# A retention block between two MoE layers: the second MoE's front moves into the last retention tiles

## The reference

```
x = x + 0.5 * moe(layernorm(x))                # MoE "a"
x = x + attn(layernorm(x))                     # retention, two layers
x = x + 0.5 * moe(layernorm(x))                # MoE "b", the same weights as "a"

moe(h): probs = softmax(h @ router_w + bias); top 2 of 16, weights normalised to sum 1
        15 experts: silu(h @ gate_w[e]) * (h @ up_w[e]) @ down_w[e]; the 16th gives h itself
        shared = silu(conv3(h)) * (h @ shared_up) @ shared_down    # causal, 3 taps
        returns shared + routed
attn(x): twice: x += retention(layernorm(x)) gated by silu, projected out
                x += gelu(layernorm(x) @ ffn1 + b1) @ ffn2 + b2
         then a final layernorm with gain and bias
```

## Time and profile before

| | |
|---|---|
| median of 3 runs | 1481.09 us (1480.42 to 1487.93) |
| profiled execution | 1481.23 us, of which span 1479.1 us |
| busy in the span | PE 1323.7 us (89%), DVE 1018.2 (69%), POOL 636.3 (43%), ACT 597.0 (40%) |
| mean granted clock of TensorE | 0.96 |

### The profile page before, as it was taken

How to read it: one execution, slowest core, us unless ns; L and a number is a source line. 1 busy time by engine, 2 the same in 40 slices (tenths; PEclk the granted TensorE clock), 3 DMA queues, 4 the chain that set the end, 5 groups by cost and what they waited for, 6 DMA issues and landing times. The chain is left out here.

```text
span 1479.1 us, 30591 instructions
## 1 busy us (share of the span) xinstructions
PE 1323.7 (89%) x11824; PEld 1086.4 (73%) x11824; DVE 1018.2 (69%) x2373; ACT 597.0 (40%) x1009; POOL 636.3 (43%) x509
## 2 busy tenths in 40 slices
PE   3899999658999999999998999999999849899994
PEld 2468996346878878888887887887887724799952
DVE  5854564768778778778768778778867667546634
ACT  6325665211443343443442433334334462356620
POOL 4766413722333134224334334633643466746045
PEclk9899999768999999999999999999999969999997
DMA  9987765710000000001010000000000051668544
GB/s 333 362 280 247 235 206 187 231 37 1 2 1 2 1 2 1 2 2 33 8 37 28 1 2 16 16 1 16 16 15 2 29 186 68 221 232 249 166 154 138
DMA packets 109323, 139.18 MB, mean 94 GB/s; under 512 B 11776, under 2 KB 95616, under 8 KB 109184
## 3 DMA queue, kind: packets, MB, share of 16 engines
q1 hardware_dynamic: 94784, 101.56, 21.1%
q0 software_dynamic: 12288, 33.57, 6.8%
q10 hardware_dynamic: 2112, 2.10, 0.4%
HBM read 71.66 MB, written 65.54 MB: 93 GB/s over the span
## 5 line engine op out<-in xcount | busy, mean ns | idle before, releaser
L1624 DVE TENSOR_TENSOR l_probs<-l_banks,l_past 128x512 f32<-128x512 f32 x256 | 159.9, 681 | 34.3 <-PE l_banks L1850 34.2
L1478 POOL TENSOR_TENSOR l_g_lo<-l_q,l_g_hi 128x1024 fp32r<-128x1024 f32 x16 | 38.4, 2398 | 285.1 <-ACT l_g_hi L1390 285.1
L1399 ACT ACTIVATE l_act_f<-l_w_ps,l_ffn_b 128x512 f32<-128x512 f32 x120 | 82.7, 689 | 176.2 <-PE l_w_ps L81 170.5
L79 PE MATMUL l_w_ps<-l_w_hi,l_f_hi 128*128 128x256 f32 x496 | 142.9, 288 | 3.6 <-DVE l_f_lo L1655 2.2
L80 PE MATMUL l_w_ps<-l_w_lo,l_f_hi 128*128 128x256 f32 x496 | 138.5, 279 | 0.0
L81 PE MATMUL l_w_ps<-l_w_hi,l_f_lo 128*128 128x256 f32 x496 | 138.4, 279 | 0.0
L597 POOL DMA_INDIRECT a_picked<-rows,a_pos_i x64 | 65.4, 1022 | 90.9 <-issue 68.4
L1465 POOL TENSOR_TENSOR l_q_wide<-l_q,l_pair_mask 128x1024 f32<-128x1024 f32 x32 | 60.1, 1898 | 100.5 <-DVE l_q L1602 100.5
L1655 DVE TENSOR_TENSOR l_f_lo<-l_act_f,l_f_hi 128x512 fp32r<-128x512 f32 x128 | 86.3, 703 | 24.1 <-ACT l_f_hi L1400 24.1
L79 PE MATMUL l_w_ps<-l_b_hi,l_w_hi 128*128 128x512 f32 x240 | 102.7, 428 | 0.0
L597 POOL DMA_INDIRECT b_picked<-rows,b_pos_i x64 | 61.5, 961 | 93.8 <-issue 68.5
(11 more groups left out here) (400 smaller groups left out, 4057.5 us busy)
## 6 DMA issues: line engine op xcount, KB each, us to landing
rows<-a_zeros SPq DMA_DIRECT2D x15, 1024.0 KB, 13.6
a_xb<-rows SPq DMA_DIRECT2D x46, 256.0 KB, 3.1
rows<-a_yb SPq DMA_DIRECT2D x46, 256.0 KB, 3.1
b_xb<-rows SPq DMA_DIRECT2D x46, 256.0 KB, 3.4
rows<-b_yb SPq DMA_DIRECT2D x46, 256.0 KB
a_w_in<-in_moe_w SPq DMA_DIRECT2D x15, 384.0 KB, 12.8
b_w_in<-in_moe_w SPq DMA_DIRECT2D x15, 384.0 KB, 9.5
l_w<-in_ffn_w SPq DMA_DIRECT2D x8, 512.0 KB, 6.4
```

The lines of the kernel that those rows point to most:

```text
L79: tensor.matmul(out, w_hi, x_hi, start=start, stop=False)
L1399: nc.scalar.activation(act_f[:, f, :], hidden_ps(b, f), ACT.Gelu, bias=ffn1_b[:, b.layer, f:f + 1]).then_inc(act_done, 1)
L1624: dve.tensor_tensor(probs[c % 2][:, r * w:(r + 1) * w].rearrange("p (h n) -> p h n", n=P), banks[:, r, :].rearrange("p (h n) -> p h n", n= ...
```

## The change

`moe` for "b" no longer has a block of its own. It returns one generator per engine, and retention's code of that engine steps it at fixed places (`next(moe)`) and runs the rest behind its own last instruction. One `hand_back` stands behind both; the barrier between them is gone. What b waits for of retention is handed over as semaphores (`held`).

The plan of b differs from that of a, which is as before: `PARTS` (16, 16), so 46 + 46 blocks; three tiles instead of four have their shared network ahead of the pairs and five in the tail; 16 columns are picked and combined beside the pairs and 16 (32 gathers) in the tail. Tiles 0 to 3 are routed first, inside retention; tiles 4 to 7 are routed in one go ahead of the first block pair.

Where the pieces of b stand:
- step 13: `statistics` 0, 1 on DVE between `low_feed` 3, 4 and 5; step 14: `statistics` 2, 3 there, then `invert(0)`;
- step 15, the last full one: `normalise` 0 to 3 on ACT in the feed, `statistics(4)` on DVE; on PE `turn` 0 and 1, `project_out`, `turn` 2 and 3, `feed_out` s 1, `route(0)`, `feed_out` s 2, `turn_logits(0)`, and only then `turn_b`; on DVE `soften(0)` ahead of the low half of b; on ACT evacuations and three `high_weights` ahead of its high half;
- last step: `tables`, `share(0)`, `choose` twice, `mark`, `statistics(5)` between the eight `low_feed`; `count(0)` on PE after `feed_out` s 0; `plan(0)`, `place(0)`;
- the final norm of tile 14 moves from POOL to DVE (`finish_nearly_last`);
- all high parts of b's weights are made by ACT, of the low ones 12 by DVE (4 before) and 3 by POOL (11 before).

`rows` are enlarged to (62, 74) blocks, so MoE "a" clears 12 blocks of 128 KB more, in two more DMAs. In b's tail the last columns are combined ahead of `add_shared(7)`, which is done in four parts.

```diff
+PLAN_A = plan_of((12, 20), 4, 8, A_BATCHES, A_BATCHES, (range(0, 1), range(1, 3), range(3, 5), range(5, 8)))
+PLAN_B = plan_of((16, 16), 3, 6, (range(0, 4), range(4, 8)), (range(0, 4),) + tuple(range(t, t + 1) for t in range(4, 8)),
+                 (range(0, 4), range(4, 6), range(6, 8)))
+ROWS = [max(plan.nblks[b] + plan.parts[b] for plan in (PLAN_A, PLAN_B)) for b in range(HALVES)]
```

VectorE, retention's last step:

```diff
                     if a is None:
                         for f in range(KF):
                             low_feed(b, f)
                             if f == 0:
                                 measure_final(after(b, -1))
+                            if f in (1, 2, 4, 6):
+                                next(moe)
+                        next(moe)
+                        finish_nearly_last(after(b, -1))
+                        next(moe)
                         for s in range(SUB):
                             measure_last(s)
...
                         finish_last(SUB - 1)
+                        run(moe)
```

TensorE, retention's last full step:

```diff
+                    if more == 0:
+                        feed_out(b, range(0, 1))
+                        next(moe)
+                        project_out(a, last_state)
+                        next(moe)
+                        feed_out(b, range(1, 2))
+                        next(moe)
+                        feed_out(b, range(2, 3))
+                        next(moe)
+                        turn_b(a)
+                        feed_out(b, range(3, SUB))
+                        return
```

The end of retention, and the calls of the three stages:

```diff
-        hand_back(nc, sems)
+        hand_back(nc, sems + next_moe.sems)
...
-        ffn("a", ins["x"], x_dram)
-        retention(nc, x_sb, ident, eps, ins, x_dram, home)
-        ffn("b", None, out)
+        ffn("a", ins["x"], x_dram, PLAN_A)
+        retention(nc, x_sb, ident, eps, ins, x_dram, home, ffn("b", None, out, PLAN_B), held)
```

1788 lines of the change are left out of this document (1073 added, 715 removed).

## The result

| | before | after |
|---|---|---|
| median of 7 runs each, one chip | 1481.22 us (1475.66 to 1487.93) | 1471.71 us (1468.51 to 1473.71) |
| profiled execution | 1481.23 us, span 1479.1 | 1473.71 us, span 1471.8 |
| busy PE, DVE, POOL, ACT | 1323.7, 1018.2, 636.3, 597.0 | 1328.2, 1019.0, 610.7, 606.4 |
| mean granted clock of TensorE | 0.96 | 0.961 |

The ratio is 0.9933, with a 95% interval of 0.9916 to 0.995: 9.5 us or 0.7% faster, just outside the 0.5% that I had called no change (the interval ends at 0.5%). The profiled execution of the kernel after is the slowest of its seven, so its trace shows 7.3 us of span less and not 9.5.

A forecast was written before the change was run, and what follows sets the result against it. Before its TensorE-filled block pairs, the second MoE was taken to pay 85 us in a chain over all engines. Terms -13.1 + 1 - 2.6 + 2 + 0.5 = -12.2 took 1481.2 to 1469.0 us; range 1456 to 1486.

The forecast's parts named there:

- sign of being wrong: Step 15 growing by more than 15 us, or the granted clock in the front staying under 0.7.
- rival (2): The gain shrinks through VectorE waits, contention at 5 us, half clock, tail and clears: 1478.5 us; chance 0.24.
- Start: Two more clears, 1.5 MB, at the start, partly taken by the DMA's free fifth of 10 us: 2 us later.
- rival (4): The clears do not hide and hold back the first MoE, nothing else differs: 1471.5 us, in the forecast's range.
- Step 14: Two statistics between the low halves put 2 x 1.75 = 3.5 us on the path.
- Step 15: TensorE inserts 8.7 us plus evacuate wait 1.1, less 2.7 of idle cover: 7.1; high half of b 0.5 more.
- Last step: Routing between the eight low halves: 9.2 us of VectorE work plus 1.3 contention, less 3.9 idle: 6.6 later.
- From the last low half to the first gate/up: VectorE's queue with 12 us of waits sets this stretch; first gate/up at about 1260, 13.1 us earlier.
- Half clock: TensorE idles 8 us before turn(4) and then runs at the lower clock level: 1 us added to the front.
- Rival (1): Granted clock stays at its lower level through the whole front, +20 us for the +1: 1488 us; chance 0.14.
- Pairs: The 46 block pairs stay at 146 us; 16 combines in the loop for 12 cost 0.
- Tail and end: Tail with 32 gathers for 40 but five shared tiles: 2.6 us earlier; semaphores cleared together at the end: 0.5 later.

The follow-up runs named there:

- the combination: Changed kernel with added clears behind pairs 8 and 14 of MoE a, GpSimd's low weights behind its first scatter, low_x ahead of weigh(1): 1471.68 us.

## Why the prediction was right, and where its terms were off

The forecast was 1469.0 us with faster, by over 0.5%, at 0.63; the median came to 1471.71, ratio 0.9933. The mechanism is the one told: the retention steps get longer, what stands behind them gets shorter by more (19.5 and 27.1 us), and without the interleaving the gain is gone. The sum had 12.2 us, the profiled executions differ by 7.3, the medians by 9.5. The 4.9 missing in the traces are: start 2.8, last steps 1.8, front 2.7, pairs 0.8, and 3.2 back from the tail and the end. That the median came within 3 us has a share of luck: in the cuts terms went 10.4 us the one way and 5.6 the other.

Most signs that I had named came late. The last low half is 24.2 us later on the clock of the trace and not 15 to 19, the positions of the first half come at 1202.82 and not 1195, TensorE's last retention matmul ends at 1208.9 and not about 1200, VectorE has one wait over 5 us (6.30), and the first gate/up falls at 1270.26 and not at 1255 to 1264. The pairs (146.8), the last gather (40.25 behind the first) and the clock in the front came as told, and neither sign of being wrong showed. In rival (2) the terms add up to 1479.0 and not 1478.5; nothing hangs on it.

**Start, 2 forecast, 4.8 measured** (up to step 14). The step failed where it gave the clears the "free fifth of 10 us". The first part of the sum, 1.5 MB at 345 GB/s or 4.5 us, was the right number by itself. TensorE shows it ahead of the first turn of a block, where it waits for the load that stands behind the clears:

```profile
98.21 1.61 PE L1279 MATMUL a_t_ps<-ident,a_xb 128*128 128x128 f32 x8 [4.61 <-DMA a_xb<-rows]
```

The same place in the combination, which has the two clears later:

```profile
93.93 1.16 PE L1288 MATMUL a_t_ps<-ident,a_xb 128*128 128x128 f32 x8 [0.44 <-DMA a_xb<-rows]
```

GpSimd's wait for the clears ahead of the second part's scatter is no sign of it: it is 7.89 us in the kernel after and 7.64 in the combination. This is the mechanism of rival (4), rightly priced. That the median of 1471.71 lies by its 1471.5 is luck, for its condition, that nothing else differs, did not hold.

**Step 14, 3.5 forecast, 3.41 measured.** Right, and it goes when the statistics go. Behind the last normalising they cost nothing that shows.

**Step 15, 7.6 forecast with the wait of the high half, 5.3 measured up to `turn_b`.** The cover was right: TensorE's idle time in the stretch is 3.7 us before; now 0.9 of it is left, and 1.0 is new, the wait for `evacuate` that I had at 1.1. The term that was off is the inserts: TensorE's busy time grows by 7.1 us and not 8.7, for `route(0)` takes about 1.9 us in all (1160.68 to 1162.6) and I had counted that twice. Before and after:

```profile
1088.28:1152.49 64.21, 60.54 (x624) 52.05 (x623) 48.87 (x115) 22.48 (x32) 33.93 (x24) 1.00 0.03 10
1096.47:1165.96 69.49, 67.59 (x678) 57.95 (x677) 50.87 (x126) 35.09 (x58) 36.64 (x29) 0.98 0.13 41
```

**Last step, 6.6 forecast, 10.8 measured** from `turn_b` to the last low half (7.1 forecast with the 0.5 for the high half, which falls here). This is the step that was off most. The same events cut it in both traces:

| piece | before | after | change |
|---|---|---|---|
| `turn_b` to the start of `l_b_lo` | 3.79 | 5.80 | +2.0 |
| `l_b_lo` | 1.23 | 2.47 | +1.2 |
| its end to the first low half | 3.05 | 4.33 | +1.3 |
| the first low half | 0.69 | 2.90 | +2.2 |
| its end to the start of the last | 9.81 | 13.83 | +4.0 |

The last piece is the inserts net of VectorE's idle time, 4.0 where I had 5.3: their arithmetic holds. The second and the fourth are contention, 3.45 us on the path where I took 1.3 and named 5 as the bound (with the 1.50 of L873, which `l_b_hi` covers, it is 4.95). I had put it at the eight operations of the two choices, which kept their 0.42 to 0.43; it sat at operations before them, two of which are retention's own. The Trainium skill, page "SBUF — State Buffer", section "Who interferes with whom", has a VectorE instruction with two SBUF inputs contend with a GpSimd instruction that reads SBUF. The trace agrees with the rule (2.47 and 2.90 for 1.23 and 0.69), at other operations than the choices; with the bound of 5 that I took for it the sum was 1472.7.

The first piece is ScalarE's queue, 2.0 where I had 0.5. Its three high parts had waited for their weights and started when `l_full` was nearly ready, and `l_b_hi` stands behind them:

```profile
1168.47 2.31 ACT L599 ACTIVATE b_w_hi<-b_w_in 128x768 fp32r<-128x768 f32 x3 [5.21 <-DMA b_w_in<-in_moe_w]
1170.69 1.04 ACT L1729 ACTIVATE l_b_hi<-l_full 128x1024 fp32r<-128x1024 f32 x1
```

The third had no term at all. TensorE idles 4.45 us for the late `l_b_lo` and starts the first `feed_in` at half clock, six matmuls at 0.63 us for 0.40; over the twelve the granted clock is 0.63:

```profile
1174.29 0.79 PE L81 MATMUL l_banks<-l_b_hi,l_w_hi 128*128 128x512 f32 x1 [4.45 <-DVE l_b_lo L2026]
```

```profile
1174.20:1178.60 4.40, 4.31 (x12) 3.28 (x13) 1.21 (x3) 2.03 (x4) 4.40 (x5) 0.63 0.00 0
```

Before, the same twelve matmuls ran at 1.00:

```profile
1157.50:1160.50 3.00, 2.94 (x12) 2.18 (x12) 1.14 (x2) 1.49 (x4) 2.55 (x2) 1.00 0.01 3
```

With step 14 and step 15 the last `l_f_lo` is 19.5 us late in the cuts and not 17.7 (and 24.2 on the clock of the trace, with the start's 4.8).

**From the last low half to the first gate/up, 72.3 forecast (with 1 for the clock), 74.97 measured.** The positions of the first half are ready at 1202.82, 7.5 after the start of the last low half where I had put 6.7, and the scatters run to 1247, off the path as told. The term that was off is the 12 us of waits of VectorE. In the trace of after they are 15.7: 6.30, 3.03, 1.37, 0.48 and 4.48, of which the first, the second and the last stand here:

```profile
1228.94 0.69 DVE L950 TENSOR_TENSOR b_sh<-b_sg,b_gu_ps 128x512 f32<-128x512 f32 x1 [6.30 <-ACT b_sg L611]
1232.66 1.83 DVE L943 TENSOR_TENSOR b_w_lo<-b_w_in,b_w_hi 128x768 fp32r<-128x768 f32 x2 [3.03 <-ACT b_w_hi L599]
...
1260.53 1.23 DVE L962 SCALAR_TENSOR_TENSOR x_sb<-b_acc_ps,x_sb 128x1024 f32<-128x1024 f32 x1 [4.48 <-PE b_acc_ps L1266]
```

The last comes from the other direction: TensorE has nothing until VectorE's `b_both`, then does `count(1)` and only then the `shared_down` for which VectorE waits:

```profile
1255.51 0.40 PE L1226 MATMUL b_low_ps<-b_blank,b_ones 128*128 128x255 bf16 x1 [6.72 <-DVE b_both L894]
...
1270.26 0.57 PE L81 MATMUL b_gu_ps<-b_w_hi,b_bx_hi 128*128 x1 [5.51 <-DVE b_bx_lo L968]
```

**Half clock, 1 forecast, up to 2.9 measured.** TensorE idles before `turn(4)` as foreseen, and pays:

```profile
1214.54 1.94 PE L1194 MATMUL b_t_ps<-ident,b_xn_middle 128*128 128x128 f32 x8 [5.69 <-DVE l_mv L2061]
1216.28 1.92 PE L1194 MATMUL b_gu_ps<-ident,b_xn_middle 128*128 128x128 f32 x8
1218.12 3.09 PE L1206 MATMUL b_low_ps<-b_xT,b_rw 128*32 128x512 f32 x8
```

Two turns at the lower of the two levels, 1.2 and not 2.4 GHz, 1.94 and 1.92 for 1.09, and most of the first routing, 3.09 for 1.91: 2.9 us. From the first `shared_in` on it is full speed (5.42 for its twelve matmuls, as before in rows 3). Rival (1) had 20 us by the clock staying low through the front; the windows above have 0.96 from 1216 to 1245. The Trainium skill, "TensorE: Matmul & The Clock Gate", section "HAM oscillation — how this bites in real kernels", was the rule behind it; here the gap of 5.69 us brought one stretch at the lower level, and the dip that comes again (0.86 from 1245 on) falls where TensorE waits anyway. Without the interleaving the rule is nearer the truth: 0.54 over 38 us.

**Pairs, 0 forecast, 0.8 measured.** No run tells why; over the traces on usual chips the stretch is 146.0 to 147.2.

**Tail and end, 2.1 forecast (2.6 less 0.5 for the end), 5.3 measured.** Of the 5.3 the tail itself, up to VectorE's last operation, has 2.5, as forecast, and the end the rest. The last of 32 gathers starts 40.25 us after the first (1457.32 - 1417.07), and the last shared tile is added 50.6 after it, as reckoned. VectorE's last operation in the kernel after:

```profile
1466.29 1.42 DVE L959 SCALAR_TENSOR_TENSOR x_sb<-b_acc_ps,x_sb 128x256 f32<-128x256 f32 x4 [3.94 <-PE b_acc_ps L1266]
```

Before, the last operation of VectorE ended at 1472.24 and the span at 1479.1, 6.9 later; now 1467.71 and 1471.8, 4.1 later, and 4.1 in every variant. I had added half a microsecond for the semaphores of retention being cleared with b's. No such cost is seen: 2.8 us went away there. The last four stores have 128 KB each in both kernels. What differs is that they follow the shared part and not the last combines, and that `hand_back` runs twice and not three times, the last time for the semaphores of both stages; what took the 2.8 us away is not tested.

## What to carry to other kernels

When a front is slid into the stage before it, count what the trace shows of it there as a cost of its own. Here 31 us were won against an order that by itself costs 22, and a forecast of the net alone would have hidden both. Before an operation of GpSimd is moved away from a two-input operation of VectorE, look at what stands at the new place; 3.2 of the 4.9 us came back in one piece, on the path. When an operation of TensorE's chain gets later, price the clock too: the late `l_b_lo` cost 1.3 us more in the matmuls behind it than its own delay. A transfer moved out of one full stretch into another that depends on the same DMA engines was not hidden here: 4.2 us gained at the first block were 0.8 when that MoE was over.

## What the runs showed of the hardware

- One VectorE operation with two SBUF inputs, 0.42 us by itself, took 4.99 beside three GpSimd operations in a row (5.31 together). At another place one such operation took 1.92, about the rest of a single one of the three. Why it got its turn between them there and not here is open. Where both start together, VectorE's operation kept its 1.23 and GpSimd's took 3.47 for 2.39.
- TensorE ran 40 transposes that wait for nothing at 0.11 us each and then showed over a microsecond of "issue" ahead of most. This was on a chip with slow DMA, at a place where TensorE shows "issue" without the additional work too.
- TensorE idled 4.45 us before the first `feed_in` of the last step and then ran twelve matmuls at a granted clock of 0.63 (six of them at about 0.63 us for 0.40); before the change it had idled 1.17 there and ran the same twelve at 1.00.
- Two groups of runs fell on chips that moved 152 to 159 GB/s where others moved 212 to 215 in the same loop, and the loop took 196 to 205 us for 147. The variant without interleaving is 0.5% slower than the kernel before on one of these and 1.4% on a usual chip.
- The first gate/up of one and the same kernel part fell between 103.9 and 109.7 us on those chips, and between 100.3 and 101.1 on the usual ones (without the combination's edit).
